# Moving the mixer's steps to other slots of a decoder kernel: token transposes into the out-projection, one head product per half slot

## The reference, cut to what matters

```
x = x + mixer(layernorm(x))              # a state-space mixer
x = x + attention(layernorm(x), ctx)     # 32 query heads, 8 key heads, 16 wide
x = x + experts(layernorm(x))            # 16 experts, top 2, and a shared one
```

```python
proj = xn @ W_in.T                       # z, xi (1024 each), dt (16), B and C (256 each)
xi = silu(causal_conv4(xi)); dt = softplus(dt + dt_bias)
u = (dt * mean_per_head(xi))[..., None] * B
h[t] = exp(dt * A) * h[t-1] + u[t]; y[t] = sum(h[t] * C[t])      # 16 heads, 16 states
y = (y @ W_h2i.T) * silu(z)              # "head products", then the gate
out = y @ W_out.T + residual
```

## Time and profile before

| | us |
|---|---|
| three executions, median (range) | 1396.94 (1394.41 to 1400.47) |
| the profiled execution, its own time | 1399.34 |
| its span, first to last instruction | 1397.5 |
| the stream phase, until the experts | about 0 to 990 |
| TensorE busy in the span | 1253.2 (90%) |
| VectorE, ScalarE, GpSimd busy | 694.0, 465.2, 242.0 |
| mean granted clock of TensorE | 0.952 |

### The profile page before, as it was taken

One profiled execution on the slowest core, in us unless ns is written; L12 is line 12 of the kernel. 1 busy time (PEld: TensorE's weight loads), 2 busy tenths in 40 slices (PEclk: granted clock), 3 DMA queues, 4 the chain that ended last, 5 costly groups with the idle time before them and its releaser, 6 DMA issues. The chain is left out here.

```text
span 1397.5 us, 14980 instructions
## 1 busy us (share of the span) xinstructions
PE 1253.2 (90%) x5077; PEld 515.8 (37%) x5078; DVE 694.0 (50%) x1049; ACT 465.2 (33%) x661; POOL 242.0 (17%) x420
## 2 busy tenths in 40 slices
PE   5989899998999999899999989999778999999930
PEld 2434433333434333343333333333333444444410
DVE  4634495566475546467555757665373111111125
ACT  1310334333554333455333544555211222222210
POOL 3010212110310201211210221111001111111135
PEclk9998999899999979899999999999989999999975
DMA  6322682003534102263200442000062335664247
GB/s 174 92 77 61 158 155 63 27 12 91 124 90 88 38 12 72 50 130 84 63 12 12 110 80 44 23 2 31 22 240 67 131 126 180 225 234 172 83 137 253
DMA packets 101232, 134.40 MB, mean 96 GB/s; under 512 B 13362, under 2 KB 72882, under 8 KB 98866
## 3 DMA queue, kind: packets, MB, share of 16 engines
q1 hardware_dynamic: 85778, 96.37, 26.1%
q0 software_dynamic: 6320, 20.71, 5.2%
q10 hardware_dynamic: 9072, 16.52, 3.1%
HBM read 104.34 MB, written 28.84 MB: 95 GB/s over the span
## 5 line engine op out<-in xcount | busy, mean ns | idle before, releaser
L606 DVE TENSOR_REDUCE mx<-ps_m 128x2 f32<-128x1024 f32 x256 | 313.3, 1224 | 283.7 <-PE ps_m L1029 279.9
L752 ACT ACTIVATE prob<-ps_s 128x1024 f32<-128x1024 f32 x256 | 262.2, 1024 | 433.2 <-PE ps_s L1012 433.1
L956 PE MATMUL acc<-xnT,wring 128*128 128x512 f32 x560 | 280.4, 599 | 2.4 <-DVE xz L538 1.8
L1630 PE MATMUL ps_gu<-ring,xgT 128*128 x376 | 179.2, 600 | 8.7 <-issue 6.7
L1012 PE MATMUL ps_s<-q_stack,k_stack 99*128 99x512 bf16 x512 | 157.9, 390 | 7.5 <-DMA q_stack<-mT 4.5
L1029 PE MATMUL ps_m<-k_stack,q_stack 96*128 96x512 bf16 x512 | 157.6, 389 | 5.6 <-DVE mx L606 5.2
L1445 DVE COPY xgT<-ps_x 128x512 f32<-128x512 f32 x47 | 32.5, 692 | 230.4 <-PE ps_x L1604 230.4
L1042 PE MATMUL ps_o<-prob,values 128*32 128x512 f32 x1024 | 140.7, 622 | 0.0
L956 PEld LDWEIGHTS acc<-xnT,wring 128*128 128x128 f32 x560 | 102.6, 190 | 67.3 <-issue 33.2
L1012 PEld LDWEIGHTS ps_s<-q_stack,k_stack 99*128 99x128 bf16 x512 | 36.0, 97 | 193.9 <-issue 143.0
L1630 PEld LDWEIGHTS ps_gu<-ring,xgT 128*128 128x128 f32 x376 | 67.7, 192 | 79.6 <-issue 79.6
(11 more groups left out here) (234 smaller groups left out, 1213.6 us busy)
## 6 DMA issues: line engine op xcount, KB each, us to landing
ring<-in_w_experts SPq DMA_DIRECT2D x16, 1536.0 KB, 8.7
wring<-in_w_in SPq DMA_DIRECT2D x80, 256.0 KB, 3.4
q_stack<-part_rows SPq DMA_DIRECT2D x96, 128.0 KB, 4.6
list_y<-y ACTq DMA_DIRECT2D x47, 256.0 KB, 2.0
wring<-in_w_out SPq DMA_DIRECT2D x32, 256.0 KB, 2.8
part_rows<-part SPq DMA_DIRECT2D x20, 384.0 KB, 3.2
xt<-in_x SPq DMA_DIRECT2D x16, 256.0 KB, 3.7
out<-res ACTq DMA_DIRECT2D x16, 256.0 KB, 4.0
```

Of the source, the lines that this page charges most:

```text
L606: nc.vector.tensor_reduce(mx[:, n % G, 2 * u:2 * u + 2], ps_m[:, :, :], AX.X, ALU.max).then_inc(s_max, 1)
L752: nc.scalar.activation(prob[:, slot % PROB, :, :], ps_s[:, :, :], ACT.Exp, scale=SCALE).then_inc(s_exp, 1)
L956: ins = nc.tensor.matmul(bank(b, n), weights, xnT[:, k, :], start=(k == 0), stop=(k == KD - 1))
L1630: ins = nc.tensor.matmul(ps_gu[p][:, :], xgT[:, p, k * P:(k + 1) * P], weights(own)[:, k * 2 * F:(k + 1) * 2 * F], start=(k == 0), stop=(k ...
```

## The change

The mixer's steps move to other slots, on all engines alike:

- the tokens of batch b + 1 are transposed at m = 48, 52, 56 and 60 of batch b, ahead of the first half of the out-projection's slot, into `ps_t` by `claim`, and VectorE empties it in the same slot after `maxima`. Batch 0's are done ahead of the loop;
- statistics, variances and residual of the next batch move from m 53 to 61 to m 4 to 10, its `load_x` from m 3 to m 1;
- `project_steps` moves to m 0, the groups to m 1 to 40 (a group now begins in an odd slot), and what follows them on ScalarE, VectorE, GpSimd and SP three or two slots earlier; m 41 is empty on TensorE;
- the head products stand one in each half slot, m 42 to 45; each waits for the gate of the last but one. The gates move ahead of `maxima` in VectorE's slot;
- the out-projection runs over m 46 to 61; m 62 and 63 are empty;
- the queries' chain is two slots earlier, the later query parts six slots earlier, and the reads back at -22, -18, -14 and 1 (before: -20, -14, -12 and 1). `bank` alternates over batches too, as (b + n) % 2.

The diff, cut to its core:

```diff
-    C_AT = (-23, -17, -15, -9)
-    ROWS_AT = (-21, -15, -13, -7)
-    STACK_AT = (-20, -14, -12, 1)
+    C_AT = (-25, -23, -17, -15)
+    ROWS_AT = (-23, -21, -15, -13)
+    STACK_AT = (-22, -18, -14, 1)
+    TURN_AT = (48, 52, 56, 60)
+    H2I_AT, OUT_AT = 42, 46
+        def bank(b, n):
+            return four[n % 4] if b == 0 else acc[(b + n) % 2][:, :]
+        H_BANK, OUT_BANK = GROUPS, GROUPS + KI
...
                 b, m = mixing(slot)
                 n, u = divmod(slot, UNITS)
+                if b < B:
+                    for i in range(KI):
+                        if m == H2I_AT + (i + 1) // 2:
+                            gate(b, i)
                 if 0 <= slot + AHEAD < SLOTS:
                     maxima(slot + AHEAD)
...
-                    if m >= 14 and m % 2 == 0 and (m - 14) // 2 < KI:
-                        taps(b, (m - 14) // 2)
-                    if m >= 17 and m % 2 == 1 and (m - 17) // 2 < KI:
-                        silu_xi(b, (m - 17) // 2)
-                    if m == 34:
+                    if m >= 11 and m % 2 == 1 and (m - 11) // 2 < KI:
+                        taps(b, (m - 11) // 2)
+                    if m >= 14 and m % 2 == 0 and (m - 14) // 2 < KI:
+                        silu_xi(b, (m - 14) // 2)
+                    if m == 32:
...
-                    if m >= 31 and m % 2 == 1 and (m - 31) // 2 < 7:
-                        silu_z(b, (m - 31) // 2)
-                    if m == 44:
+                    if m >= 28 and m % 2 == 0 and (m - 28) // 2 < 7:
+                        silu_z(b, (m - 28) // 2)
+                    if m == 41:
                         silu_z(b, 7)
...
-                    if m in (52, 56, 60):
-                        add_x1(b, (m - 52) // 4)
+                    if m in (50, 54, 58, 62):
+                        add_x1(b, (m - 50) // 4)
...
+                        if m in TURN_AT:
+                            evacuate(b + 1, TURN_AT.index(m))
...
             def transpose_tokens(b, j):
                 pe.wait_ge(s_ln, TB * b + j + 1)
                 if b:
-                    pe.wait_ge(*((s_x1, TB * b - 1), (s_x1, TB * b), (s_xnT, TB * b + 1), (s_xnT, TB * b + 2))[j])
+                    claim(s_xnT, TB * b + j + 1)
+                turned = four[j] if b == 0 else ps_t[:, :]
...
-            def heads_to_inner(b, p):
-                if p == 0:
-                    pe.wait_ge(s_zs, KI * (b + 1))
+            def heads_to_inner(b, i):
+                if i == 0:
                     pe.wait_ge(s_ysb, b + 1)
...
-                for i in (2 * p, 2 * p + 1):
-                    r = 32 * (i % 4)
-                    ins = nc.tensor.matmul(bank(b, i), wh2i[r:r + H, i * P:(i + 1) * P], ysb[r:r + H, :],
-                                           start=True, stop=True, tile_position=(r, 0))
-                ins.then_inc(s_h2i, 1)
+                pe.wait_ge(s_zs, KI * b + min(KI, KI - 1 + i))
+                if i >= 2:
+                    pe.wait_ge(s_gate, KI * b + i - 1)
+                r = 32 * (i % 4)
+                nc.tensor.matmul(bank(b, H_BANK + i), wh2i[r:r + H, i * P:(i + 1) * P], ysb[r:r + H, :],
+                                 start=True, stop=True, tile_position=(r, 0)).then_inc(s_h2i, 1)
...
             def mixer_half(b, m, h):
-                if m < 2:
-                    transpose_tokens(b, 2 * m + h)
-                elif m < 4:
-                    if 2 * m + h == 4:
-                        project_steps(b)
-                elif m < 44:
-                    project(b, m // 2 - 1, 2 * (m % 2) + h)
-                elif m < 48:
-                    if h:
-                        heads_to_inner(b, m - 44)
-                else:
-                    project_out(b, (m - 48) // 4, 2 * (m % 4) + h)
+                at = 2 * m + h
+                if at == 0:
+                    project_steps(b)
+                elif 2 <= at < 4 * GROUPS - 2:
+                    project(b, (m + 1) // 2, 2 * ((m - 1) % 2) + h)
+                elif 2 * H2I_AT <= at < 2 * H2I_AT + KI:
+                    heads_to_inner(b, at - 2 * H2I_AT)
+                elif 2 * OUT_AT <= at < 2 * OUT_AT + TB * KI:
+                    j, i = divmod(at - 2 * OUT_AT, KI)
+                    project_out(b, j, i)
```

More of the change, by code:

```diff
@@ L496, in _ @@
             steps = Steps(dve, s_v)
-            def bank(b, n):
-                return four[n % 4] if b == 0 else acc[n % 2][:, :]
             def statistics(b, j):
@@ L559, in gate @@
             def gate(b, i):
-                dve.wait_ge(s_h2i, 4 * b + i // 2 + 1)
-                nc.vector.scalar_tensor_tensor(out=gated[i], in0=bank(b, i), scalar=0.5, in1=gated[i],
+                dve.wait_ge(s_h2i, KI * b + i + 1)
+                nc.vector.scalar_tensor_tensor(out=gated[i], in0=bank(b, H_BANK + i), scalar=0.5, in1=gated[i],
                                                op0=ALU.mult, op1=ALU.mult).then_inc(s_gate, 1)
@@ L566, in add_x1 @@
                 slot = x1[:, b * TB + j, :]
-                nc.vector.tensor_tensor(slot, bank(b, j), slot, ALU.add).then_inc(s_x1, 1)
+                nc.vector.tensor_tensor(slot, bank(b, OUT_BANK + j), slot, ALU.add).then_inc(s_x1, 1)
             def scan(b, k):
@@ L662, in _ @@
                 residual(0, j)
+            for j in range(TB):
+                evacuate(0, j)
             for slot in span:
@@ L705, in _ @@
[L705 to L709 removed]
+                    if m in (37, 38):
+                        scan(b, m - 37)
+                    if m in (50, 54, 58, 62):
+                        add_x1(b, (m - 50) // 4)
                     if b + 1 < B:
[L711 to L713 removed]
+                        if 4 <= m <= 7:
+                            statistics(b + 1, m - 4)
+                        if m == 8:
@@ L719, in _ @@
                 for j in range(TB):
-                    if (a := batch_at(slot, -39 + 4 * j)) is not None:
+                    if (a := batch_at(slot, -41 + 4 * j)) is not None:
                         attention_statistics(a, j)
-                if (a := batch_at(slot, -26)) is not None:
+                if (a := batch_at(slot, -28)) is not None:
                     attention_variances(a)
-                if (a := batch_at(slot, -25)) is not None:
+                if (a := batch_at(slot, -27)) is not None:
@@ L725, in _ @@
                     normalise(a, 0)
                     normalise(a, 1)
-                if (a := batch_at(slot, -24)) is not None:
+                if (a := batch_at(slot, -26)) is not None:
                     normalise(a, 2)
@@ L847, in _ @@
                         nc.scalar.activation(th[:, i % 2, :], bank(b, 13 + i), ACT.Tanh, scale=0.5).then_inc(s_thz, 1)
-                if b < B and m == 43:
+                if b < B and m == 40:
                     act.wait_ge(s_y, b + 1)
@@ L917, in transpose_tokens @@
                 if b:
-                    pe.wait_ge(*((s_x1, TB * b - 1), (s_x1, TB * b), (s_xnT, TB * b + 1), (s_xnT, TB * b + 2))[j])
+                    claim(s_xnT, TB * b + j + 1)
+                turned = four[j] if b == 0 else ps_t[:, :]
                 for k in range(KD):
-                    ins = nc.tensor.transpose(bank(b, j)[:, k * P:(k + 1) * P], xt[:, j, k * P:(k + 1) * P],
-                                              ident[:, :])
+                    ins = nc.tensor.transpose(turned[:, k * P:(k + 1) * P], xt[:, j, k * P:(k + 1) * P], ident[:, :])
                 ins.then_inc(s_tr, 1)
@@ L976, in project_out @@
                 if j == 0:
-                    if i == 0:
-                        pe.wait_ge(s_gate, KI * (b + 1))
+                    if i in (0, KI - 1):
+                        pe.wait_ge(s_gate, KI * b + (KI if i else KI - 1))
                     pe.wait_ge(s_w[w % RING], 16 * (w // RING + 1))
+                if i == 0 and j == 1:
+                    pe.wait_ge(s_gate, KI * (b + 1))
                 if b and j >= 2 and i == 0:
                     pe.wait_ge(s_x1, TB * b + j - 1)
-                ins = nc.tensor.matmul(bank(b, j), gated[i][:, j * P:(j + 1) * P], ring[:, w % RING, :],
+                ins = nc.tensor.matmul(bank(b, OUT_BANK + j), gated[i][:, j * P:(j + 1) * P], ring[:, w % RING, :],
                                        start=(i == 0), stop=(i == KI - 1))
@@ L1104, in _ @@
             pe.wait_ge(s_ident, 16)
+            for j in range(TB):
+                transpose_tokens(0, j)
             for slot in span:
@@ L1118, in _ @@
                     transpose_max(n + 1)
-                if b < B and m == 34:
+                if b < B and m == 32:
                     head_means(b)
-                if b < B and m == 42:
+                if b < B and m == 40:
                     outputs(b)
+                if b + 1 < B and m in TURN_AT:
+                    transpose_tokens(b + 1, TURN_AT.index(m))
                 if b < B:
```

95 lines of the change are left out of this document (38 added, 57 removed).

## The result

The changed kernel takes 1428.07 us (median of four runs, 1424.81 to 1429.65) where the kernel before, measured beside it, takes 1395.68 (1392.61 to 1400.47): a ratio of 1.0226, with a 95% interval of 1.0179 to 1.0274. It is slower. The forecast was 1392, the range ended at 1408. The profiled execution took 1424.8 us, 25.5 more than the profiled one of before (1399.3).

A forecast was written before the change was run, and what follows sets the result against it. TensorE was taken as the bound, busy 1253.2 of 1397.5 us, so only its waits and clock pay. Terms summed to 15.2 us faster without falls, 4 us with one: 1396.9 to 1392.7, stated as 1392, range 1374 to 1408.

The forecast's parts named there:

- The turn of the batch: m 0 to 3 of a batch: moving the transposes removes waits and lower clock, 17.1 us less new waits, gain 10.9 us.
- The claims on the small bank: Transposes of m 48 and 56 claim `ps_t`, so the maxima's transposes behind wait 0.9 us each, 3.6 us in all.
- The wait of 0.8 us at m 13: Moved statistics and residual crowd VectorE in batch 2: one wait of 0.8 us, bounds 0 and 2.
- The wait for the exponential where no mixer step covers it (m 62): Batch end without mixer steps: scores of 63 wait for the exponential of 62, 0.9 us in each of batches 1 to 3.
- The waits for `silu_z`: Projection groups 15 to 20 now wait for `silu_z`: 4.5 us in each of batches 1 to 3, loss 13.5 us.
- The sign that I named: Profile row expected if right: the projection's waits for `silu_z` show about 4.9 us a batch.
- The late transfer: Third read-back of queries: moving it ends the scores' 4.2 us wait and 2 us of lost clock, gain 6.2 us.
- The lead-in: Ahead of the batches: its turn gains 2.2 us, its clock fall in the head stage loses 2.7 us.
- Head products at an unchanged clock: Single products cost 2.9 us more a batch, the lost 1.9 us wait offsets: nothing, between +1 and -1.5 us a batch.
- The clock in the head stage: Head stages: the 1.9 us wait goes, gain 13 us, less 11 for each fall that comes back; one fall taken.
- The slower rival: Two or three falls at m 42 to 45, 11 us each: two give 1403.7, three 1414.7; chance 0.25.
- The rival by the Trainium skill: No fall in the head stages, since only idle gaps between matmul bursts lower the clock: 1382 us, chance 0.27.

The follow-up runs named there:

- the kernel with 64 rows: The changed kernel with each head product over 64 rows (two copies of its 16) at one of two row positions: 1391.19 us, ratio to before 0.9938.
- The control with the mask: The changed kernel with the loaded number of weights masked with 31 ahead of its wait in the experts' phase, value unchanged: 1426.38 us.

## Why the prediction was wrong

**The turn of the batch: right.** 10.9 us forecast, 13.3 by the ledger. The waits of the earlier trace rows left, m 0 to 3 hold clock 1.00. The stretch takes 13.8 us and not near 9, as I wrote under what would show it: it now holds projections from m 1 on and one group of query transposes, which the like stretch of the earlier trace rows does not. A place in the slots is no fixed piece of work once steps have moved; the ledger above allows for that. The claims on the small bank cost 0.7 us each for 0.9, at the slots named. The wait of 0.8 us at m 13 didn't come: m 9 to 13 of batch 2 have the lengths of before, but for 0.16 us at m 11. The wait for the exponential where no mixer step covers it (m 62) was 0.68 us for 0.9.

**The waits for `silu_z`: right, in place and in size.** 13.5 us forecast; 14.1 by the ledger, 14.7 when they were taken away. m 28 is 1.48 us longer than before, m 34 and 36 0.88 each, for 1.6, 0.9 and 0.9. The sign that I named was off: the rows of L952 waiting for L558 were to show 4.9 us a batch and show 8.8 in all, 2.9 a batch; the rest of the longer slots stands in no wait row.

**The late transfer: right.** 6.9 us for 6.2 in the changed kernel.

**The lead-in: sizes off, sum about right.** -1.1 for +0.5. The turn there gained what was forecast: from the end of the last out-projection to the first projection it takes 0.9 us for 4.8, and the four groups of transposes now inside the out-projection take 0.43 us each, 3.9 - 1.7 = 2.2. The wait for GpSimd ahead of the outputs' products (L905) grew from 2.8 to 4.3 us, and the clock was low for 3.4 us from 95.1 and for 10.2 from 105.4, where the kernel before had the 10.2 alone.

**Head products at an unchanged clock: wrong size.** I took 0.9 us for a single product, "0.86 us or somewhat more", and set the sum to 0. It is 1.05 us, and the pair behind takes 0.11 longer before the next product: a half slot is 1.59 us against 1.29 for a product over all rows. With the clock held, the stage takes 18.0 us in the kernel with 64 rows (whose half slots are as long), 3.3 more than the 14.7 of before, some 10 us in three batches. The row that could have told me was the earlier trace rows: the pair at two row positions took 1.07 us, longer than one full product's 0.86, so a product at a position of its own was no cheaper than 0.86 and could be as long as the pair.

**The clock in the head stage: this step failed.** I had the mechanism in the text (thin products may not hold the clock) and priced a fall in the new stage at 11 us; 28.3 - 18.0 = 10.3 were measured. What failed is the number of falls: one in three batches, where all three fell. I let batch 3 of before speak for the change: it had held 1.00 through its four pairs, so the wait of 1.9 us had to be at least half of the cause, and taking it away had to help. The runs show the reverse of both. With the wait gone the clock fell in all three batches; with the wait left in place, products over all rows in the kernel before cut the 10.2 and 20.5 us at the lower clock in its head stages to 3.4 and none. So the wait was not what made the long falls, and of the 12.9 us that I booked as gained the head stages gave back nothing. That batch 3 had held was one draw of what differs between batches and between executions.

Against it stood the lead-in row that I quoted (0.50 for 10.2 us, TensorE busy 8.8 of them). I read that row wrongly: the pairs fill only its first 3.8 us, then come 1.4 us of idle time and 5.0 us of out-projection, and I had written that such products and a few transposes were all that ran. But the fall began 2.6 us into the pairs, and it was the stage with the least full work beside them. I took it for a special case. The change moved every head stage its way: eight half slots with a thin product, for four.

In sum: two more falls at 10.3 us and 3 x 3.3 us of longer stages give 30.5 us, and 29.7 is the miss against the profiled execution (25.5 against -4.2). The slower rival ("two or three falls", three give 1414.7) was the right one, and still 13 us short, some 10 of it for the size of the singles. The rival by the Trainium skill (TensorE: Matmul & The Clock Gate, its last table: no idle gaps between bursts of matmuls, and throughput doesn't drop) is refuted by this trace: the clock was lower in three stretches in which TensorE was busy for 23.90 of 23.90 us. Part 3 of that page of the Trainium skill says that packed small matmuls run together; the trace agrees (1.07 us for a pair). The prediction's other statement by that page of the Trainium skill, that a product of few rows costs a full one's time, does not hold here: 1.05 us for 0.86, and the measurement decides. Taking the pairs apart was a pure loss, as the prediction said that it would be by that page, of 3.3 us a batch at the upper clock for 2.9.

**Left open.** The last 3.1 us, after the mixer: the experts' phase has the same work and order, and its first lower stretch is 13.7 us long for 6.8 before. The control with the mask has 6.8 us there, and from its last pair of maxima to the end it takes 434.3 us, where the changed kernel took 436.5 and the kernel before 433.5. So 2.2 of these us came with the longer fall of that one execution and are no cost of the change as far as this shows. Nor was it found out where between 16 and 64 rows the clock begins to hold, or what decides which stage of paired thin products falls in an execution.

## What to carry to other kernels

A busy TensorE does not by itself keep its clock: where a stage is full of matmuls over a few rows, look at the granted clock of that stage, and try rows of zero weights (15.8 us for 28.3 here, and 43 us of 1426 by one edit). Before you spread packed small matmuls over time, count how long one takes alone, since a pair side by side costs what one does. A batch that holds the clock in one profile proves nothing while its neighbours with the same work do not. Look at the times and clocks of many executions first, and price a change that makes such a stage thinner with a fall in every one.

## What the runs showed of the hardware

- Products over 16 of 128 rows, one in each half slot beside a full pair of bf16 products, lower the clock to 0.50 for 23.9 us with TensorE busy throughout. Over 64 rows, or over 128 of which 112 hold zero weights, it stays at 1.00.
- A product at a row position of its own makes its half slot 0.30 us longer than the same product over all rows (1.59 against 1.29 us), at 16 rows and at 64, at the upper clock.
- A product padded to all rows is shorter than the thin product that it replaces (0.86 against 1.05 us), and rows of zero weights give the same head stage as copies (15.8 us). It costs only where thin products had run side by side (17.8 us for 14.7).
- Falls of paired thin products differ between equal stages and between executions: head stages of 19.4, 22.9 and 14.7 us in the profile before, 19.4, 14.7 and 22.7 in the one with a transfer moved, and times from 1390.39 us at a mean clock of 0.959 to 1407.72 at 0.948 for the one unchanged kernel.
